# Shift operations on GpSimd instead of VectorE, two native slots in stage 0, and new engine orders, in a two-layer attention kernel

## The chip, the cores and the metric

The kernel runs on 1 core of a Trainium2 chip. The metric is the device time of one execution in microseconds (us), lower is better. Engines are named as in the profile: PE (TensorE), DVE (VectorE), ACT (ScalarE), POOL (GpSimd), SP (the queue that issues the DMAs).

## The reference

Two self-attention layers follow each other on `x` of shape 4 x 128 x 32 x 32, so 4 images of 128 channels and N = 1024 positions. Layer 1 has weights of its own and takes what layer 0 gives.

```python
q = einsum('rc,bcn->brn', Wq, xf) + bq[None, :, None]      # 16 rows
k = einsum('rc,bcn->brn', Wk, xf) + bk[None, :, None]      # 16 rows
v = einsum('oc,bcn->bon', Wv, xf) + bv[None, :, None]      # 128 rows
attn = softmax(einsum('bri,brj->bij', q, k), axis=2)       # 1024 x 1024
out = einsum('bcj,bij->bci', v, attn)
return gamma * out + x
```

## The kernel before

**Stages.** There are 8 stages: stage s is image s % 4 of layer s // 4. Stage s + 4 reads what stage s wrote to `x_all`. In a stage the 1024 x 1024 scores are made twice, in 8 tiles of 128 x 1024 each time.

**First pass (E).** `energies` (L633) makes a tile of scores with queries in the rows, `row_max` (L522) takes the negated maximum of each row on DVE, and `row_sums` (L430) takes the exponential and its row sums on ACT. `log_sums` (L436) takes the logarithm of the sums.

**The shift.** The shift of a row is its negated maximum less the logarithm of its sum. With it added to the scores, an exponential gives finished softmax weights. `cut_shift` (L527) makes it on DVE: L539 subtracts (128 x 8 elements, one column for each tile), L542 rounds the result to the short format fp32r, L544 subtracts the rounded part from the whole. The three depend on one another through semaphores. `transpose_shift` (L648) turns the two parts on PE into rows (L655), `shift_to_rows` (L546) copies them from PSUM on DVE (L553), and `place_shift` (L308) writes them by two small DMAs into spare rows of the stage's query and key tensors. In stage 0 the shift is made in two halves, of four tiles each. The first half isn't placed by a DMA but added by small matmuls (L674, L676).

**Second pass (ET).** `energies_transposed` (L657) makes the scores again, transposed and with the shift included; `attention` (L442) takes their exponential into `attn` on ACT. A tile of it is called a slot.

**Products.** Slots 0 and 7 of each stage are native: `times_v` (L713) multiplies them as fp32. Stage 0 has four native slots (0, 1, 4, 7). The other slots are cut in two fp32r parts: `hi` (a rounding, L341 on POOL or L451 on ACT) and `lo` (what the rounding left, L346 on POOL or L519 on DVE). V is cut in the same way (`v_hi`: L352 or L456, `v_lo`: L358 or L515). A cut slot then takes six fp32r passes: four in `times_v_high` (PH, L707, needs `hi`) and two in `times_v` (PV, needs `lo`). `finish` (L556) adds the residual on DVE.

**Ordering.** Each engine works through a list written out by hand: `PE_ORDER` (L46), `ACT_ORDER` (L67), `DVE_ORDER` (L81), `POOL_ORDER` (L93), `SP_ORDER` (L101). An entry is operation.stage.tile; in PE's list a last number names one of three PSUM buffers (`ring`). `warm` entries are matmuls on zeros. An engine never passes an entry that waits. Semaphores count completions, and the counts are derived from the lists. `parts.s.h` in DVE's list is a call of `cut_shift`. Stage 6 and 7 (`WHOLE`) use all 128 rows of PE in a product; the others run two products of 64 rows side by side.

The stage number stands in each entry: `ET.3.*` are the slots of stage 3 and `shift.3.1` is the transposition that they depend on. Each list interleaves two to three stages.

Of the kernel before, what the change touches and what calls it, by code (L numbers as in the profile page):

```python
# [69 lines left out]
sum.2.5 attn.0.6 v_hi.1.0 attn.0.5 sum.2.2 attn.0.7 sum.2.4 attn.1.1 attn.1.2 attn.1.3 sum.2.6 hi.1.3 sum.2.3  # L70
sum.2.1 attn.1.4 log.2.1 attn.1.0 attn.1.5 sum.3.3 attn.1.6 sum.3.7 sum.3.1 attn.2.3 sum.3.5 attn.2.1 attn.1.7
v_hi.2.0 attn.2.5 sum.3.6 sum.3.2 sum.3.0 sum.3.4 log.3.1 attn.2.2 hi.2.5 attn.2.0 sum.4.7 attn.2.4 sum.4.5 attn.2.7
attn.3.2 sum.4.2 sum.4.1 attn.3.5 attn.2.6 attn.3.7 attn.3.3 sum.4.0 sum.4.6 sum.4.3 sum.4.4 sum.5.2 log.4.1
attn.3.4 hi.3.5 attn.3.1 attn.3.0 hi.3.1 sum.5.4 sum.5.7 attn.3.6 sum.5.5 attn.4.0 attn.4.1 attn.4.2 hi.4.1 attn.4.3
sum.5.1 sum.5.6 sum.5.0 sum.5.3 hi.4.3 log.5.1 attn.4.5 attn.4.4 sum.6.6 attn.4.6 sum.6.4 attn.4.7 attn.5.0 attn.5.2
sum.6.1 attn.5.3 attn.5.1 attn.5.5 sum.6.2 sum.6.3 sum.6.7 sum.6.0 attn.5.4 sum.6.5 sum.7.5 log.6.1 sum.7.0 attn.5.6
sum.7.1 attn.5.7 sum.7.6 sum.7.4 attn.6.1 attn.6.3 attn.6.2 attn.6.4 sum.7.7 sum.7.3 attn.6.7 hi.6.1 sum.7.2 log.7.1
attn.6.0 attn.6.5 attn.6.6 hi.6.5 hi.6.6 attn.7.2 attn.7.5 hi.7.2 attn.7.6 attn.7.4 attn.7.7 hi.7.5 attn.7.3
attn.7.1 attn.7.0
# [2 lines left out]
max.0.7 max.0.3 v32.0.0 max.0.5 max.0.4 max.0.0 max.0.2 max.0.1 max.1.6 parts.0.0 max.0.6 rows.0.0 mask.2.0
stack.2.0 parts.0.1 max.1.2 rows.0.1 max.1.1 max.1.3 max.1.5 max.1.0 max.1.4 max.1.7 max.2.7 max.2.0 max.2.5
parts.1.1 v32.1.0 rows.1.1 max.2.2 finish.0.0 max.2.4 mask.3.0 stack.3.0 max.2.6 max.2.3 max.2.1 finish.0.1 v32.2.0
parts.2.1 max.3.3 rows.2.1 max.3.7 max.3.1 max.3.5 finish.1.0 mask.4.0 stack.4.0 max.3.6 max.3.2 max.3.0 max.3.4
# [715 lines left out]
```

## Time and profile before

| | us |
|---|---|
| median of 3 runs | 213.25 |
| lowest and highest | 212.74, 218.13 |
| profiled execution | 212.72 |
| span of its trace | 210.9 |
| what lies around the span | 1.8 |
| mean granted clock of PE (1 is full) | 0.984 |

The span is 1.8 us shorter than the timed execution. Times in rows are us from the start of the span. A group of instructions has its busy time, the mean of one in ns, and the idle time of the engine just before them with what ended it. A row of windows has the length of the window, then PE, PEld (PE's weight loads), DVE, ACT and POOL busy with their number of instructions, PE's granted clock as a share of full speed, DMA share and GB/s.

### The profile page before, as it was taken

How to read it: one execution, taken by the hardware profiler on the slowest of the kernel's cores; microseconds unless marked ns; L12 is line 12 of the kernel's file. 1: busy time of each engine (PE TensorE's matmuls, PEld its weight loads, DVE VectorE, ACT ScalarE, POOL GpSimd, SP SyncE). 2: the span in 40 equal slices, each digit the busy share in tenths (PEclk: the TensorE clock that was granted, in tenths of full speed). 3: DMA queues.
4: the chain of work that ended last, by engine and by line, in shares of the span. 5: the costliest groups of instructions: out<-in, count | busy, mean ns of one | idle time of the engine just before them, and what ended most of it. 6: DMA issues, size and time to landing. Idle time of an engine off the chain costs nothing.

```text
span 210.9 us, 3123 instructions
## 1 busy us (share of the span) xinstructions
PE 187.4 (89%) x1107; PEld 121.6 (58%) x1109; DVE 168.8 (80%) x162; ACT 153.3 (73%) x219; POOL 149.1 (71%) x95
## 2 busy tenths in 40 slices
...
GB/s 166 364 17 177 22 103 2 0 3 3 51 50 2 6 0 99 3 3 0 101 3 3 0 78 26 0 3 53 99 50 0 33 23 50 3 5 14 86 49 51
DMA packets 3871, 9.49 MB, mean 45 GB/s; under 512 B 545, under 2 KB 913, under 8 KB 3857
## 3 DMA queue, kind: packets, MB, share of 16 engines
...
q8 instruction: 9, 0.15, 0.3%
...
HBM read 2.89 MB, written 2.10 MB: 24 GB/s over the span
## 4 chain that ended last, share of the span: by engine, by line
PE 61%; DVE 21%; ACT 7%; issue 4%; POOL 3%; DMA 2%; SPq 0%; DVEq 0%; POOLq 0%
PE out_psum L692 25%; PE out_psum L690 5%; PE ring L667 5%; PE ring L619 5%; PE ring L643 5%; ACT ring L433 5%; DVE shift_parts L542 5%; PE ring L629 5%; DVE attn_lo L519 5%; DVE shift L539 4%; PE out_psum L693 3%; PE out_psum L726 3%; DVE shift_parts L544 3%; DVE x_all L567 2%; DVE neg_max L524 2%
## 5 line engine op out<-in xcount | busy, mean ns | idle before, releaser
L524 DVE TENSOR_REDUCE neg_max<-ring 128x1 f32<-128x1024 f32 x64 | 76.1, 1220 | 17.5 <-PE ring L645 17.1
L433 ACT ACTIVATE ring<-ring,neg_max 128x1024 f32<-128x1024 f32 x64 | 69.6, 1087 | 19.6 <-DVE neg_max L524 19.5
L346 POOL TENSOR_TENSOR attn_lo<-attn,attn_hi 128x1024 fp32r<-128x1024 f32 x34 | 81.9, 2418 | 2.6 <-ACT attn_hi L451 1.8
L445 ACT ACTIVATE attn<-ring 128x1024 f32<-128x1024 f32 x64 | 63.7, 1025 | 15.5 <-PE ring L669 13.1
L341 POOL TENSOR_SCALAR attn_hi<-attn 128x1024 fp32r<-128x1024 f32 x35 | 39.1, 1124 | 39.8 <-ACT attn L445 36.0
L643 PE MATMUL ring<-qk_swapped,qk 64*128 64x512 f32 x56 | 26.6, 481 | 3.0 <-ACT ring L433 2.4
L669 PE MATMUL ring<-qk_swapped,qk 64*128 64x512 f32 x64 | 28.0, 467 | 0.0
L667 PE MATMUL ring<-qk,qk_swapped 64*128 64x512 f32 x64 | 27.6, 461 | 0.3 <-DVE shift_rows L553 0.2
L645 PE MATMUL ring<-qk,qk_swapped 64*128 64x512 f32 x56 | 27.0, 488 | 0.0
L693 PE MATMUL out_psum<-attn,v 64*128 64x512 f32 x56 | 26.4, 591 | 0.0
L692 PE MATMUL out_psum<-attn,v 64*128 64x512 f32 x56 | 26.4, 591 | 0.0
L519 DVE TENSOR_TENSOR attn_lo<-attn,attn_hi 128x1024 fp32r<-128x1024 f32 x12 | 22.0, 1855 | 0.4 <-ACT attn_hi L451 0.4
L693 PE MATMUL out_psum<-attn_hi,v_hi 64*128 64x512 f32 x68 | 22.1, 405 | 0.0
L692 PE MATMUL out_psum<-attn_hi,v_hi 64*128 64x512 f32 x68 | 22.1, 404 | 0.0
L692 PE MATMUL out_psum<-attn_lo,v_hi 64*128 64x512 f32 x68 | 21.5, 416 | 0.0
L693 PE MATMUL out_psum<-attn_lo,v_hi 64*128 64x512 f32 x68 | 21.5, 415 | 0.0
L692 PE MATMUL out_psum<-attn_hi,v_lo 64*128 64x512 f32 x68 | 21.5, 396 | 0.0
L693 PE MATMUL out_psum<-attn_hi,v_lo 64*128 64x512 f32 x68 | 21.4, 395 | 0.0
L667 PEld LDWEIGHTS ring<-qk,qk_swapped 64*128 64x128 f32 x64 | 11.4, 188 | 11.4 <-issue 9.7
L643 PEld LDWEIGHTS ring<-qk_swapped,qk 64*128 64x128 f32 x56 | 10.8, 192 | 12.4 <-issue 10.1
L358 POOL TENSOR_TENSOR v_lo<-v,v_hi 128x768 fp32r<-128x768 f32 x8 | 16.6, 2081 | 0.7 <-ACT v_hi L456 0.6
L629 PEld LDWEIGHTS ring<-late,x_all 128*128 128x128 f32 x128 | 14.9, 191 | 3.7 <-issue 3.7
...
## 6 DMA issues: line engine op xcount, KB each, us to landing
...
qk<-shift_rows SPq DMA_DIRECT2D x7, 8.0 KB
```

The lines of the kernel that those rows point to most:

```text
L341: nc.gpsimd.tensor_scalar(attn_hi[:, k - 1], attn[:, k], 1.0, 0.0, ALU.mult, ALU.add).then_inc(cut_made["hi", "gpsimd"], 1)
L346: nc.gpsimd.tensor_tensor(attn_lo[:, k - 1], attn[:, k], attn_hi[:, k - 1].bitcast(fp32), ALU.subtract).then_inc(cut_made["lo", "gpsimd"], 1)
L433: nc.scalar.activation(e[:], e[:], ACT.Exp, bias=neg_max[s][:, i:i + 1], accum_out=row_sum[s][:, i:i + 1]).then_inc(sum_made, 1)
L445: nc.scalar.activation(attn[:, k], ring_tile("ET", s, k)[:].rearrange("p (a n) -> p a n", a=2), ACT.Exp).then_inc(attn_made, 1)
L519: nc.vector.tensor_tensor(attn_lo[:, k - 1], attn[:, k], attn_hi[:, k - 1].bitcast(fp32), ALU.subtract).then_inc(cut_made["lo", "vector"], 1)
L524: nc.vector.tensor_reduce(neg_max[s][:, i:i + 1], ring_tile("E", s, i)[:], axis=AX.X, op=ALU.max, negate=True).then_inc(max_made, 1)
L643: nc.tensor.matmul(to[:, 0:HALF], q_over_k[0:deep, rows], k_over_q[0:deep, 0:HALF], start=True, stop=True)
L645: nc.tensor.matmul(to[:, HALF:N], k_over_q[64:64 + deep, rows], q_over_k[64:64 + deep, HALF:N], start=True, stop=True).then_inc(e_mm, 1)
L667: nc.tensor.matmul(to[:, 0:HALF], k_over_q[0:64, first], q_over_k[0:64, part], start=True, stop=not added(s, h))
L669: last = nc.tensor.matmul(to[:, HALF:N], q_over_k[64:128, second], k_over_q[64:128, part], start=True, stop=not added(s, h))
L692: nc.tensor.matmul(out_psum[:, 0:HALF], v[0:64], a[0:64], start=start, stop=stop)
L693: last = nc.tensor.matmul(out_psum[:, HALF:N], v[64:128], a[64:128], start=start, stop=stop)
```

## The change

- The three shift operations are issued by GpSimd (`split_shift`) and no more by VectorE (`cut_shift`). The rounding is written as a multiplication by 1.0 with 0.0 added, as other roundings of GpSimd are. `parts` entries move from VectorE's list to GpSimd's.
- Stage 0 has two native slots (0 and 7), so its slots 1 and 4 are cut.
- The second half of stage 0's shift has a place of its own in `shift_parts` (`parts_of`).
- All five lists are written anew. In numbers of entries, before and after:

| | before | after |
|---|---|---|
| `hi` on ACT, on POOL | 11, 35 | 18, 30 |
| `lo` on DVE, on POOL | 12, 34 | 10, 38 |
| `v_hi` on ACT, on POOL | 3, 5 | 1, 7 |
| `v_lo` on DVE, on POOL | 0, 8 | 1, 7 |
| `parts` on DVE, on POOL | 9, 0 | 0, 9 |
| `PH` | 46 | 48 |
| warm-up matmuls in PE's list | 14 | 16 |

```diff
-NATIVES = [(0, 1, 4, 7), (0, 7), (0, 7), (0, 7), (0, 7), (0, 7), (0, 7), (0, 7)]
+NATIVES = [(0, 7), (0, 7), (0, 7), (0, 7), (0, 7), (0, 7), (0, 7), (0, 7)]
...
-raw.0.0.0 raw.0.1.1 QK.1.0.2 E.0.7.0 E.0.3.1 V.0.0.2 E.0.5.0 E.0.4.1 E.0.0.2 warm.0.4 E.0.2.0 E.0.1.1 E.1.6.2
-warm.0.4 E.0.6.0 warm.0.1 QK.2.0.1 shift.0.0.2 warm.0.3 ET.0.2.2 ET.0.1.0 warm.0.2 E.1.2.2 ET.0.0.1 shift.0.1.0
-PH.0.2 E.1.1.0 ET.0.3.1 E.1.3.2 PV.0.1 E.1.5.1 ET.0.4.0 E.1.0.2 PH.0.3 E.1.4.0 E.1.7.1 E.2.7.2 PV.0.3 E.2.0.0 PV.0.0
+raw.0.0.0 raw.0.1.1 E.0.7.2 E.0.0.0 QK.1.0.1 E.0.3.2 E.0.2.0 V.0.0.1 E.0.1.2 E.0.4.0 E.0.6.1 warm.0.4 E.0.5.2
+warm.0.4 shift.0.0.0 E.1.6.1 E.1.7.0 warm.0.2 QK.2.0.2 ET.0.3.1 ET.0.2.0 warm.0.1 ET.0.1.1 shift.0.1.2 E.1.2.0
+E.1.0.2 V.1.0.1 warm.0.1 ET.0.0.0 E.1.3.2 ET.0.4.1 warm.0.2 E.1.4.0 warm.0.2 E.1.5.1 PH.0.3 E.1.1.2 PH.0.2 E.2.4.0
...
-ET.7.1.1 ET.7.3.2 PH.7.6 PH.7.5 PH.7.4 PH.7.2 PV.7.7 PV.7.6 PV.7.5 PV.7.4 PH.7.1 PH.7.3 PV.7.2 PV.7.1 PV.7.3 PV.7.0
+ET.7.5.0 ET.7.4.2 ET.7.7.1 PH.7.3 PH.7.6 PH.7.1 PV.7.0 PH.7.4 PH.7.5 PV.7.1 PV.7.4 PH.7.2 PV.7.6 PV.7.2 PV.7.3
+PV.7.5 PV.7.7
...
 DVE_ORDER = """
...
-rows.7.1 lo.6.1 lo.6.6 lo.6.3 finish.6.1 finish.6.0 lo.7.2 lo.7.6 lo.7.4 lo.7.1 finish.7.1 lo.7.3 finish.7.0
+max.7.4 finish.5.1 v32.7.0 rows.7.1 lo.6.3 lo.6.4 finish.6.0 finish.6.1 lo.7.1 lo.7.3 lo.7.6 lo.7.4 finish.7.0
+finish.7.1
...
 POOL_ORDER = """
-mask.1.0 stack.1.0 v_lo.0.0 hi.0.2 lo.0.2 hi.0.3 lo.0.3 hi.0.6 lo.0.6 hi.0.5 v_lo.1.0 lo.0.5 hi.1.1 lo.1.1 hi.1.2
...
-lo.6.5 v_lo.7.0 hi.7.6 hi.7.4 lo.7.5 hi.7.1 hi.7.3
+mask.1.0 stack.1.0 v_hi.0.0 parts.0.0 parts.0.1 v_lo.0.0 lo.0.2 hi.0.3 lo.0.3 hi.0.1 v_hi.1.0 hi.0.4 v_lo.1.0
+parts.1.1 lo.0.4 hi.0.5 lo.0.5 lo.0.6 hi.1.2 hi.1.3 lo.1.2 hi.1.5 hi.1.1 lo.1.1 hi.1.6 lo.1.3 parts.2.1 lo.1.6
...
+hi.5.4 hi.5.6 v_hi.6.0 lo.5.6 lo.5.4 hi.6.1 hi.6.3 lo.6.5 parts.7.1 v_hi.7.0 lo.6.1 v_lo.7.0 lo.6.2 lo.6.6 hi.7.6
+hi.7.3 hi.7.2 hi.7.5 lo.7.2 lo.7.5
 """
 SP_ORDER = """
-swap.1.0 swap.0.0 swap.2.0 place.0.1 place.1.1 swap.3.0 place.2.1 swap.4.0 place.3.1 swap.5.0 place.4.1 swap.6.0
+swap.1.0 swap.0.0 place.0.1 swap.2.0 place.1.1 swap.3.0 place.2.1 swap.4.0 place.3.1 swap.5.0 place.4.1 swap.6.0
...
+        def parts_of(s, h):
+            return shift_parts[s][:, 2 * tiles_of(s, h).start:2 * tiles_of(s, h).stop]
...
+            def split_shift(s, h):
+                tiles = tiles_of(s, h)
+                part, count = slice(tiles.start, tiles.stop), len(tiles)
...
+                pool.wait_ge(max_made, all_of(nth_max, s, tiles))
+                pool.wait_ge(log_made, nth_log[s, h])
+                nc.gpsimd.tensor_tensor(shift[s][:, part], neg_max[s][:, part], log_sum[s][:, part],
+                                        ALU.subtract).then_inc(shift_made, 1)
+                pool.wait_ge(shift_made, nth_parts[s, h])
+                nc.gpsimd.tensor_scalar(hi, whole, 1.0, 0.0, ALU.mult, ALU.add).then_inc(shift_hi_made, 1)
+                pool.wait_ge(shift_hi_made, nth_parts[s, h])
+                nc.gpsimd.tensor_tensor(lo, whole, hi.bitcast(fp32), ALU.subtract).then_inc(shift_cut, 1)
```

## Rows read from the trace of the kernel before

**Rows 1.** The page: busy time of each engine.
```profile
PE 187.4 (89%) x1107; PEld 121.6 (58%) x1109; DVE 168.8 (80%) x162; ACT 153.3 (73%) x219; POOL 149.1 (71%) x95
```
**Rows 2.** The page: the chain that ended last, shares by line.
```profile
PE out_psum L692 25%; PE out_psum L690 5%; PE ring L667 5%; PE ring L619 5%; PE ring L643 5%; ACT ring L433 5%; DVE shift_parts L542 5%; PE ring L629 5%; DVE attn_lo L519 5%; DVE shift L539 4%; PE out_psum L693 3%; PE out_psum L726 3%; DVE shift_parts L544 3%; DVE x_all L567 2%; DVE neg_max L524 2%
```
**Rows 3.** The waits, whole span: total us, times, longest.
```profile
POOL attn_hi L341 <- ACT attn L445: 36.0, 7, 9.4
ACT ring L433 <- DVE neg_max L524: 19.5, 15, 3.4
...
PE ring L655 <- DVE shift_parts L544: 13.8, 6, 3.0
```
**Rows 4.** DVE's groups by form: the three shift operations in stages 1 to 7.
```profile
L542 DVE CAST shift_parts<-shift 128x8 fp32r<-128x8 f32 x7 | 10.0, 1429 | 0.2
...
L539 DVE TENSOR_TENSOR shift<-neg_max,log_sum 128x8 f32<-128x8 f32 x7 | 6.9, 987 | 1.3 <-ACT log_sum L440 1.1
L544 DVE TENSOR_TENSOR shift_parts<-shift,shift_parts 128x8 fp32r<-128x8 f32 x7 | 3.3, 476 | 0.2
```
**Rows 5.** Timelines around three shifts: start, duration, instruction.
```profile
27.95 1.05 POOL L341 TENSOR_SCALAR attn_hi<-attn 128x1024 fp32r<-128x1024 f32 x1 [9.41 <-ACT attn L445]
28.11 0.89 DVE L539 TENSOR_TENSOR shift<-neg_max,log_sum 128x4 f32<-128x4 f32 x1
29.07 2.34 POOL L346 TENSOR_TENSOR attn_lo<-attn,attn_hi 128x1024 fp32r<-128x1024 f32 x1
29.24 2.19 DVE L544 TENSOR_TENSOR shift_parts<-shift,shift_parts 128x4 fp32r<-128x4 f32 x1
...
46.34 0.16 DVE L539 TENSOR_TENSOR shift<-neg_max,log_sum 128x8 f32<-128x8 f32 x1
46.74 0.17 DVE L544 TENSOR_TENSOR shift_parts<-shift,shift_parts 128x8 fp32r<-128x8 f32 x1
...
131.18 0.20 ACT L440 ACTIVATE log_sum<-row_sum 128x8 f32<-128x8 f32 x1
...
135.97 0.22 PE L655 MATMUL ring<-units,shift_parts 128*16 128x128 f32 x1 [2.98 <-DVE shift_parts L544]
```
**Rows 6.** Windows: three that cover POOL's work, and two at a low clock.
```profile
28.00:113.00 85.00, 74.04 (x487) 50.56 (x488) 73.70 (x76) 69.40 (x103) 62.80 (x38) 0.98 0.11 26
113.00:163.00 50.00, 44.16 (x302) 30.58 (x300) 43.78 (x42) 39.52 (x57) 48.90 (x29) 0.99 0.12 33
163.00:202.40 39.40, 37.86 (x199) 25.93 (x198) 31.52 (x25) 27.71 (x35) 26.69 (x16) 0.97 0.08 28
...
33.00:36.00 3.00, 3.00 (x20) 2.44 (x20) 1.63 (x2) 1.74 (x4) 0.00 (x0) 0.56 0.01 3
162.00:165.00 3.00, 3.00 (x17) 2.10 (x14) 1.97 (x4) 2.60 (x4) 1.55 (x1) 0.50 0.05 11
```
**Rows 7.** POOL's groups by form, from the largest operation to the smallest.
```profile
L346 POOL TENSOR_TENSOR attn_lo<-attn,attn_hi 128x1024 fp32r<-128x1024 f32 x34 | 81.9, 2418 | 2.6 <-ACT attn_hi L451 1.8
...
L358 POOL TENSOR_TENSOR v_lo<-v,v_hi 128x768 fp32r<-128x768 f32 x8 | 16.6, 2081 | 0.7 <-ACT v_hi L456 0.6
L352 POOL TENSOR_SCALAR v_hi<-v 128x768 fp32r<-128x768 f32 x5 | 4.2, 831 | 2.9 <-DVE v L509 2.9
...
L394 POOL TENSOR_SCALAR units<-units 128x640 fp32r<-128x640 f32 x1 | 0.7, 717 | 0.0
...
L794 POOL MEMSET const-float32-0.0<- 128x1 f32 x1 | 0.1, 98 | 0.2 <-issue 0.2
```
**Rows 8.** Timeline of the end, DVE and PE.
```profile
191.74 1.99 PE L690 MATMUL out_psum<-attn_lo,v_hi 128*128 128x512 f32 x8
...
194.64 8.79 DVE L519 TENSOR_TENSOR attn_lo<-attn,attn_hi 128x1024 fp32r<-128x1024 f32 x4
...
204.01 1.21 DVE L519 TENSOR_TENSOR attn_lo<-attn,attn_hi 128x1024 fp32r<-128x1024 f32 x1
...
205.84 1.88 PE L690 MATMUL out_psum<-attn,v 128*128 128x512 f32 x4
```

116 lines of the change are left out of this document (52 added, 64 removed).

## The prediction

> **What bounds the kernel now.** I read the busy times first, then the chain that ended last, the waits, and last the timeline around the places they name.
>
> PE is busy 187.4 of 210.9 us, DVE 168.8, ACT 153.3, POOL 149.1 [rows 1]. No engine is full, so what counts is what PE waits for: 23.5 us of the span it does nothing. The chain consists of PE work for the most part, but 12% of it is DVE's three shift operations: 5% L542, 4% L539, 3% L544, some 25 us [rows 2]. Those work on 8 columns. The waits say the same from PE's side: 13.8 us in six waits of the transposition L655 for L544, up to 3.0 us [rows 3]. That is by far PE's largest wait for another engine.
>
> Why do operations on 8 columns take 1429, 987 and 476 ns in the mean [rows 4]? In stage 1, with POOL idle, the first and the last take 0.16 and 0.17 us. In stage 0, L539 starts at 28.11 during a POOL rounding that ends at 29.00 and itself ends at 29.00; L544 starts at 29.24, during POOL's `lo` that ends at 29.07 + 2.34 = 31.41, and ends at 31.43 [rows 5]. So the DVE operation stands still until the running POOL operation is over. Three dependent operations can meet three POOL operations in turn. From the end of the logarithm at 131.38 to the transposition at 135.97 it takes 4.6 us in stage 5, and PE is idle for the last 3.0 of them [rows 5].
>
> POOL is the second thing to watch. From 28 to 202.4 it is busy 62.8 + 48.9 + 26.7 = 138.4 us and idle 36.0: 22.2 before 113, 1.1 in 113 to 163, 12.7 after [rows 6]. In the middle it is 98% busy. Its idle time is waiting for `attn` (36.0 in 7 waits [rows 3], the first, 9.4, before 28 [rows 5]), and `attn` comes late where PE stood at a shift.
>
> **The change part by part.** All sums are made against the profiled execution, 212.72 us = span 210.9 + 1.8 around it; it lies 0.5 below the median of 213.25, at the low end of the runs.
>
> *1. The shift leaves DVE.* Removed from DVE are 9 x 3 operations; the seven stages with 8 columns alone are 10.0 + 6.9 + 3.3 = 20.2 us [rows 4]. DVE isn't the bound, but ACT waited 19.5 us for DVE's maxima [rows 3], so a part of this helps ACT as well.
>
> *2. The shift on POOL.* No POOL operation on 8 columns is in the trace. Upper end: the smallest ones with two inputs and with one, 2081 and 717 ns, so 2 x 2.08 + 0.72 = 4.9 us for the three. Lower end: three at the 98 ns of the one-column memset, 0.3 us [rows 7]. Between them I draw lines through two sizes: with one input 717 ns at 640 columns and 831 at 768 give 0.89 ns a column and 150 ns at none. With two inputs, 2081 at 768 contains some waiting for DVE; 2418 at 1024 gives 1.3 ns a column and then 1070 ns at none. The `lo` rows that meet no DVE operation take 2.34 [rows 5], which is 2.3 ns a column if nothing stands at none. I take 250 ns, nearest to the one-input line, since nothing says that an operation on 8 columns costs half of one on 1024. So 0.25 + 0.15 + 0.25, with 0.1 in each gap: 0.85 us. Before it come the remains of a POOL operation, some 0.8 us, half of 149.1 / 95 [rows 1]. From logarithm to transposition that is 1.7 us in place of up to 4.6, so a PE wait of 13.8 / 6 = 2.3 us nearly vanishes. I keep 0.5 for each of 7 stages. On PE: -13.8 + 3.5 = -10.3.
>
> The Trainium skill (GPSIMD Engine Reference, section 4.1, Engine selection) speaks against this move: elementwise work belongs on VectorE, GpSimd being about twice as slow with two inputs. This trace agrees for an undisturbed operation (`lo` 1.21 on DVE [rows 8], 2.34 on POOL [rows 5]). By that rule the three would cost about 1.0 us as an estimate, from 0.16 doubled, instead of 0.85: 1.4 us over nine shifts. What the rule leaves out is the standing still seen above.
>
> *3. Behind the new waits.* While POOL waits for the logarithm, the `hi` and `lo` behind it in its list stand (`parts.2.1` has `lo.1.6` behind it), and PV on PE waits for those. Before, they ran on while DVE waited. This is the cost that rival A prices. On DVE `rows` still waits for the transposition, and SP's `place` behind it; `swap.2.0` now stands behind `place.0.1`, at most the time from stacking to that shift, covered by the E tiles of stage 1 which PE has first. I put nothing for it.
>
> *4. The clock.* The granted clock was 0.56 in 33 to 36 and 0.50 in 162 to 165 [rows 6], half speed, each time after PE had waited at a shift of stage 0 or 6. That cost 3 x 0.44 + 3 x 0.5 = 2.8 us. I count 1.7 as coming back, as the start still has gaps.
>
> *5. Two slots become cut.* A native slot is four passes in 1.88 us with its tail, some 1.72 without it [rows 8]. An fp32r pass takes 0.23 at its pace (8 in 1.99, of which some 0.16 is tail), so six take 1.4 [rows 8]. So -0.7 us on PE for two. Added are two `hi` (1.05) and two `lo` (2.34) [rows 5], 6.8 us on the other engines, in the stretch where POOL idles longest (22.2 us in 28 to 113). Cover gone, they would cost at most these 6.8.
>
> *6. New lists.* POOL gets 4 `lo` more, 5 `hi` fewer, 2 `v_hi` more, 1 `v_lo` fewer and 9 shifts: 4 x 2.34 - 5 x 1.05 + 2 x 0.83 - 2.08 + 9 x 0.85 = +11.3 us. ACT gets 7 `hi` more and 2 `v_hi` fewer, 7 x 1.05 - 2 x 0.83 = +5.7. DVE loses two `lo` and gains a `v_lo`. The first loads stay as they are. The `hi` of ACT is priced as that of POOL.
>
> **The sum, from two sides.** PE's side: 210.9 - 10.3 - 1.7 - 0.7 = 198.2 of span, 200.0 us, if no new wait appears. POOL's side: of the +11.3, 2.5 (a `v_hi` and two shifts) fall before 28, so it works 138.4 + 8.8 = 147.2 us from 28 on. Behind its last entry, `lo.7.5`, follow what followed the last `lo` before, which ended at 205.22: two passes, a native slot, `finish`, the store; 210.9 - 205.2 = 5.7. With its idle time of 36.0 unchanged this is 28 + 147.2 + 36.0 + 5.7 = 216.9, so 218.7 us. But the idle time is what the stalls at the shifts made. Six waits fewer, of which about four reached POOL, at 2.3 each: -9. Work for the two cut slots in the idle start: -5. Leaves 22: 202.9 of span, 204.7 us. The later side rules. Forecast **204.7 us**.
>
> **The rivals.**
>
> *A, slower: POOL's queue.* POOL idles as long as before: what it saves where `attn` now comes earlier it loses standing at `parts` for the logarithm with work queued behind. That is the sum above, 218.7 us. For it: 98% busy in 113 to 163, and 11.3 us more work. Against it: ACT gives `attn` late because of PE's stalls, which go. It decides at an idle time of 30.0 us from 28 on, where the sum is 212.7.
>
> *B, about the same: new waits.* The stalls of PE go, but half of the gain turns into waits for `hi` and `lo`, since ACT has 5.7 and POOL 11.3 us more to do. Half of what separates 204.7 from 218.7: 211.7 us. For it: the end of the kernel, where four `lo` on DVE took 8.79 us and not 4 x 1.21 because POOL was working [rows 8]; POOL has six `lo` in the last two stages, four before. Against: the middle stages have PE at full pace but for the shifts.
>
> The Trainium skill says in Perfetto Trace Analysis, Optimizing Scalar/DVE Operations, that moving work between these two engines might not help, since they share a port. By that rule B is the case to expect; rows 5 show such a sharing, and that what it costs three short operations in a chain is more than their own time, which moving them does save.
>
> *C, faster: PE's side rules.* No new wait: 200.0 us, and 210.9 - 13.8 - 2.8 - 0.7 + 1.8 = 195.4 with all of it coming back. For it: POOL's idle total is large. Against: each list has been full of dependences, and something is next.
>
> *D: the shift on POOL is as dear as the upper end.* 4.9 in place of 0.85 us, 9 times: 36 us more on POOL, over 230 us. By the two-input line, 1.07 twice, it is 1.6 us more a shift, +15 on POOL, and 212 with half of that on the path. Only the end far from the rows of small operations gives it.
>
> **How the numbers follow.** Forecast (202 to 209): 0.50. C (below 202): 0.16. B (209 to 217): 0.22. A, with D's far end: 0.12, of which 0.09 is above 217.5. The range reaches from 199 to 213.5 and leaves some 0.05 below and 0.15 above. A measurement of this kernel can tell about 2% (4.3 us) from no change: faster than 209.0 is 0.50 + 0.16 = 0.66, within 2% 0.22 + 0.03 = 0.25, slower 0.09.
>
> **What would show it.** The wait of L655 for another engine falls from 13.8 to under 5 us, on POOL now. The three operations on POOL are 0.2 to 0.3 us each with no idle stretch of PE over 1 us at a shift. DVE's busy time falls to about 143 (20.2 and stage 0's part less, two `lo` less), POOL's rises to about 160, ACT's to 159. POOL idles about 22 us from 28 to its last entry. No window at half clock after 100. I am wrong if POOL stands at `parts` for over 1 us a stage, if the three take over 1.5 us, or if PE has new waits for `hi` or `lo` of over 6 us in sum.

## The result and the profile after

| | before | after |
|---|---|---|
| median, us (4 runs each, taken together) | 215.69 | 202.44 |
| lowest and highest | 212.74, 218.13 | 201.81, 202.95 |
| profiled execution, its span | 212.72, 210.9 | 201.81, 200.0 |
| mean granted clock | 0.984 | 0.974 |

The ratio is 0.9503, 95% interval 0.9445 to 0.9562: 5% faster. It leaves out executions of the kernel before with a disturbed clock, so it is nearer to 1 than the quotient of the medians. The forecast was 204.7 us in a range of 199 to 213.5, so time and direction came as predicted. The parts of the sum did not.

The page of the kernel after, busy time and chain by engine and by line; it answers to [rows 1, 2]:

```profile
PE 187.7 (94%) x1117; PEld 123.9 (62%) x1119; DVE 144.8 (72%) x134; ACT 157.2 (79%) x224; POOL 160.5 (80%) x122
...
POOL 40%; PE 36%; DVE 10%; issue 8%; ACT 4%; POOLq 0%; ACTq 0%
POOL attn_lo L352 25%; PE ring L649 7%; PE out_psum L698 7%; POOL attn_hi L347 7%; DVE attn_lo L546 5%; PE out_psum L732 5%; POOL v_lo L364 5%; PE out_psum L696 4%; DVE neg_max L551 4%; PE ring L625 4%; PE ring L673 3%; PE ring L635 2%; ACT ring L460 2%; PE ring L613 2%; ACT attn L472 1%
```

PE is busy as long as before (187.7 against 187.4 us) in 11 us less of span. None of the three shift lines is among the fifteen that the page names any more; the chain goes through POOL's `lo` (25%) and `hi` (7%) now. Lines have moved: L539, L542, L544 are L379, L382, L384; the transposition L655 is L661.

The waits of the kernel after (total us, times, longest), against [rows 3]:

```profile
ACT ring L460 <- DVE neg_max L551: 14.4, 13, 3.5
...
POOL attn_lo L352 <- ACT attn_hi L478: 6.7, 2, 5.1
POOL shift L379 <- ACT log_sum L467: 6.5, 2, 3.6
POOL attn_hi L347 <- ACT attn L472: 5.3, 4, 1.6
...
PE out_psum L696 <- POOL attn_lo L352: 1.1, 1, 1.1
PE out_psum L696 <- DVE attn_lo L546: 1.0, 1, 1.0
PE out_psum L698 <- DVE attn_lo L546: 0.9, 1, 0.9
...
PE ring L661 <- POOL shift_parts L384: 0.3, 1, 0.3
```

PE's 13.8 us at the shift are 0.3. POOL's 36.0 for `attn` are 5.3. Its waits for the `hi` of ACT are 6.7 where they were 1.8, and 6.5 for the logarithm are new. PE's waits for `lo` are three, 3.0 us in sum, where they were 0.7.

POOL's groups by form, and a shift in the timeline of the kernel after (start, duration, instruction), against [rows 4, 5]:

```profile
L379 POOL TENSOR_TENSOR shift<-neg_max,log_sum 128x8 f32<-128x8 f32 x7 | 2.5, 352 | 0.0
L384 POOL TENSOR_TENSOR shift_parts<-shift,shift_parts 128x8 fp32r<-128x8 f32 x7 | 1.4, 206 | 0.6
L382 POOL TENSOR_SCALAR shift_parts<-shift 128x8 fp32r<-128x8 f32 x7 | 1.4, 204 | 0.6
```

```profile
145.74 1.04 POOL L347 TENSOR_SCALAR attn_hi<-attn 128x1024 fp32r<-128x1024 f32 x1
146.75 0.20 POOL L379 TENSOR_TENSOR shift<-neg_max,log_sum 128x8 f32<-128x8 f32 x1
147.04 0.20 POOL L382 TENSOR_SCALAR shift_parts<-shift 128x8 fp32r<-128x8 f32 x1
147.33 0.21 POOL L384 TENSOR_TENSOR shift_parts<-shift,shift_parts 128x8 fp32r<-128x8 f32 x1
147.49 4.76 POOL L352 TENSOR_TENSOR attn_lo<-attn,attn_hi 128x1024 fp32r<-128x1024 f32 x2
```

The three take 0.79 us from 146.75 to 147.54, with a POOL operation directly on either side. On DVE they took 2.9 us of busy time in the mean [rows 4]. The mean of 352 for L379 comes from one of 1.19 us, which met a `lo` of DVE:

```profile
45.36 2.86 DVE L546 TENSOR_TENSOR attn_lo<-attn,attn_hi 128x1024 fp32r<-128x1024 f32 x1
47.09 1.19 POOL L379 TENSOR_TENSOR shift<-neg_max,log_sum 128x8 f32<-128x8 f32 x1
```

The `lo` ends at 48.22 and the shift's subtraction at 48.28. So the standing still works in both directions; POOL's subtraction met it once in nine shifts.

Windows of the kernel after: three that cover POOL's work from 28 us on, against [rows 6], and two in the start; behind them the same two of the kernel before:

```profile
28.00:113.00 85.00, 81.64 (x543) 54.98 (x545) 70.56 (x68) 79.61 (x119) 76.05 (x57) 0.99 0.11 27
113.00:163.00 50.00, 48.87 (x364) 38.12 (x362) 42.17 (x42) 44.67 (x65) 47.84 (x33) 1.00 0.13 39
163.00:193.80 30.80, 28.66 (x133) 19.05 (x130) 18.53 (x13) 20.39 (x23) 26.25 (x16) 1.00 0.07 27
...
12.00:15.00 3.00, 3.00 (x6) 0.94 (x4) 1.57 (x2) 2.34 (x4) 0.90 (x2) 0.55 0.00 0
24.00:27.00 3.00, 3.00 (x8) 0.90 (x8) 1.05 (x2) 1.52 (x5) 0.61 (x3) 0.50 0.59 143
```

```profile
12.00:15.00 3.00, 3.00 (x24) 2.16 (x20) 2.46 (x3) 2.08 (x3) 2.92 (x3) 1.00 0.00 0
24.00:27.00 3.00, 3.00 (x23) 1.62 (x21) 2.76 (x4) 1.97 (x6) 0.00 (x0) 1.00 0.00 0
```

POOL is busy 76.05 + 47.84 + 26.25 = 150.1 us from 28 on and idle 15.7. The two rows of the start are new and bad: the granted clock was 0.55 and 0.50, where the kernel before had 1.00 in both windows. PE's 3.00 us there hold 6 and 8 instructions where they held 24 and 23.

### The profile page after: what moved, and what is told of

Read it like the earlier page. It is cut to its first block, busy times and chain, and to the rows that moved or that the text cites. A ratio compares the mean times of both kernels' runs of the same rounds, so it can differ in the third digit from the quotient of the medians.

```text
span 200.0 us, 3150 instructions
## 1 busy us (share of the span) xinstructions
PE 187.7 (94%) x1117; PEld 123.9 (62%) x1119; DVE 144.8 (72%) x134; ACT 157.2 (79%) x224; POOL 160.5 (80%) x122
## 3 DMA queue, kind: packets, MB, share of 16 engines
q1 hardware_dynamic: 3856, 9.30, 15.7%
## 4 chain that ended last, share of the span: by engine, by line
POOL 40%; PE 36%; DVE 10%; issue 8%; ACT 4%; POOLq 0%; ACTq 0%
POOL attn_lo L352 25%; PE ring L649 7%; PE out_psum L698 7%; POOL attn_hi L347 7%; DVE attn_lo L546 5%; PE out_psum L732 5%; POOL v_lo L364 5%; PE out_psum L696 4%; DVE neg_max L551 4%; PE ring L625 4%; PE ring L673 3%; PE ring L635 2%; ACT ring L460 2%; PE ring L613 2%; ACT attn L472 1%
## 5 line engine op out<-in xcount | busy, mean ns | idle before, releaser
L352 POOL TENSOR_TENSOR attn_lo<-attn,attn_hi 128x1024 fp32r<-128x1024 f32 x38 | 94.1, 2490 | 7.3 <-ACT attn_hi L478 6.7
L551 DVE TENSOR_REDUCE neg_max<-ring 128x1 f32<-128x1024 f32 x64 | 76.1, 1220 | 18.8 <-PE ring L651 18.3
L460 ACT ACTIVATE ring<-ring,neg_max 128x1024 f32<-128x1024 f32 x64 | 69.6, 1088 | 14.9 <-DVE neg_max L551 14.4
L347 POOL TENSOR_SCALAR attn_hi<-attn 128x1024 fp32r<-128x1024 f32 x30 | 32.5, 1091 | 5.9 <-ACT attn L472 5.3
L673 PE MATMUL ring<-qk,qk_swapped 64*128 64x512 f32 x64 | 26.6, 453 | 1.2 <-ACT attn L472 0.4
L649 PE MATMUL ring<-qk_swapped,qk 64*128 64x512 f32 x56 | 25.8, 465 | 1.7 <-ACT attn L472 0.7
L675 PE MATMUL ring<-qk_swapped,qk 64*128 64x512 f32 x64 | 27.0, 459 | 0.0
L651 PE MATMUL ring<-qk,qk_swapped 64*128 64x512 f32 x56 | 26.2, 471 | 0.0
L698 PE MATMUL out_psum<-attn,v 64*128 64x512 f32 x48 | 22.5, 588 | 0.0
L699 PE MATMUL out_psum<-attn,v 64*128 64x512 f32 x48 | 22.5, 588 | 0.0
L699 PE MATMUL out_psum<-attn_hi,v_lo 64*128 64x512 f32 x72 | 22.2, 388 | 0.0
L698 PE MATMUL out_psum<-attn_hi,v_lo 64*128 64x512 f32 x72 | 22.2, 387 | 0.0
L698 PE MATMUL out_psum<-attn_lo,v_hi 64*128 64x512 f32 x72 | 20.7, 391 | 0.9 <-DVE attn_lo L546 0.9
L546 DVE TENSOR_TENSOR attn_lo<-attn,attn_hi 128x1024 fp32r<-128x1024 f32 x10 | 20.0, 2023 | 2.0 <-ACT attn_hi L478 2.0
L699 PE MATMUL out_psum<-attn_lo,v_hi 64*128 64x512 f32 x72 | 20.6, 391 | 0.0
L575 DVE SCALAR_TENSOR_TENSOR x_all<-out_psum,weights,x_all 128x512 f32<-128x512 f32 x16 | 12.0, 751 | 9.4 <-PE out_psum L696 9.0
L478 ACT CAST attn_hi<-attn 128x1024 fp32r<-128x1024 f32 x18 | 18.6, 1044 | 0.1
```

The lines of the kernel that those rows point to most:

```text
L347: nc.gpsimd.tensor_scalar(attn_hi[:, k - 1], attn[:, k], 1.0, 0.0, ALU.mult, ALU.add).then_inc(cut_made["hi", "gpsimd"], 1)
L352: nc.gpsimd.tensor_tensor(attn_lo[:, k - 1], attn[:, k], attn_hi[:, k - 1].bitcast(fp32), ALU.subtract).then_inc(cut_made["lo", "gpsimd"], 1)
L460: nc.scalar.activation(e[:], e[:], ACT.Exp, bias=neg_max[s][:, i:i + 1], accum_out=row_sum[s][:, i:i + 1]).then_inc(sum_made, 1)
L546: nc.vector.tensor_tensor(attn_lo[:, k - 1], attn[:, k], attn_hi[:, k - 1].bitcast(fp32), ALU.subtract).then_inc(cut_made["lo", "vector"], 1)
L551: nc.vector.tensor_reduce(neg_max[s][:, i:i + 1], ring_tile("E", s, i)[:], axis=AX.X, op=ALU.max, negate=True).then_inc(max_made, 1)
L649: nc.tensor.matmul(to[:, 0:HALF], q_over_k[0:deep, rows], k_over_q[0:deep, 0:HALF], start=True, stop=True)
```

## The experiments

Two theories stood first. M: the move does it, since a short DVE operation stands still until the running POOL operation ends. L: the new lists do it. Letters in the expectations are these; what other runs were for is told with each. Ratios are to the kernel before, with 95% intervals. The kernel before, measured anew beside each run, had medians of 215.6 to 216.9 us, so runs are compared with one another by their times.

**The move alone** (e1_move_alone): the lists of before, `parts` out of DVE's and into POOL's list; the second half of stage 0's shift has its own place in `shift_parts`, as in the change.

```diff
 POOL_ORDER = """
-mask.1.0 stack.1.0 v_lo.0.0 hi.0.2 lo.0.2 hi.0.3 lo.0.3 hi.0.6 lo.0.6 hi.0.5 v_lo.1.0 lo.0.5 hi.1.1 lo.1.1 hi.1.2
+mask.1.0 stack.1.0 v_lo.0.0 parts.0.0 parts.0.1 hi.0.2 lo.0.2 hi.0.3 lo.0.3 parts.1.1 hi.0.6 lo.0.6 hi.0.5 v_lo.1.0
...
-lo.6.5 v_lo.7.0 hi.7.6 hi.7.4 lo.7.5 hi.7.1 hi.7.3
+hi.5.4 hi.5.6 lo.5.4 hi.6.3 v_hi.6.0 v_lo.6.0 hi.6.2 hi.6.4 lo.6.2 v_hi.7.0 parts.7.1 lo.6.4 lo.6.5 v_lo.7.0 hi.7.6
+hi.7.4 lo.7.5 hi.7.1 hi.7.3
```

> The lists of the kernel before, with nothing changed but that the nine shift entries leave VectorE's list and stand in GpSimd's, behind the operation that GpSimd was at when the logarithm was made. Theory M (the standing still of VectorE's three short operations was the cost, and moving them is what gains): PE's wait for the transposition falls from 13.8 us in sum to under 5, and the time to 203 to 207 us. Rival L (the new lists gain, by putting more PE work between the logarithm and the transposition): the time stays at 209 to 213, since the old PE list has PE stand at the transposition in any case.

Measured: 198.83 us (198.11 to 200.26), ratio 0.9261 [0.9181, 0.934]. The page and the waits of this kernel:

```profile
PE 185.6 (94%) x1107; PEld 121.4 (61%) x1109; DVE 147.6 (74%) x135; ACT 153.5 (77%) x219; POOL 155.5 (78%) x122
...
POOL 48%; PE 26%; issue 9%; DVE 7%; ACT 6%; DMA 2%; SPq 0%; POOLq 0%
```

```profile
POOL shift L378 <- ACT log_sum L466: 12.2, 3, 5.4
...
POOL attn_hi L346 <- ACT attn L471: 6.8, 4, 2.9
...
PE ring L660 <- POOL shift_parts L383: 4.0, 3, 2.2
```

M holds, and L falls: the gain is there with the lists of before. It is 4 us more than M's range of 203 to 207 had. The move alone is worth some 14 us (198.83 against the 213.25 of the prediction's table; 16.8 against the 215.62 measured beside it) and is faster than the whole change: no execution of the one overlaps with one of the other (198.11 to 200.26, 201.81 to 202.95). The rest of the change costs 202.44 - 198.83 = 3.6 us.

**The lists alone** (e2_lists_alone): the lists and slots of after, the three operations back on DVE as `cut_shift`, each `parts` entry at a place of my choice near the same point.

```diff
-max.0.7 max.0.0 max.0.3 max.0.2 v32.0.0 max.0.1 max.0.4 max.0.6 max.0.5 rows.0.0 max.1.6 max.1.7 mask.2.0 stack.2.0
+max.0.7 max.0.0 max.0.3 max.0.2 v32.0.0 max.0.1 max.0.4 max.0.6 parts.0.0 max.0.5 rows.0.0 parts.0.1 max.1.6
...
-mask.1.0 stack.1.0 v_hi.0.0 parts.0.0 parts.0.1 v_lo.0.0 lo.0.2 hi.0.3 lo.0.3 hi.0.1 v_hi.1.0 hi.0.4 v_lo.1.0
+mask.1.0 stack.1.0 v_hi.0.0 v_lo.0.0 lo.0.2 hi.0.3 lo.0.3 hi.0.1 v_hi.1.0 hi.0.4 v_lo.1.0 lo.0.4 hi.0.5 lo.0.5
```

> The kernel after with only the move undone: its lists, with the nine shift entries taken from GpSimd's list and put in VectorE's, each at the place where VectorE was when the logarithm was made. Theory M: the three operations take 2 to 3 us a stage on VectorE again (their means 500 to 1400 ns), and 5 us or more of the gain are lost, 207 us or above. Rival L: the new PE list has 2.5 to 7 us of work between logarithm and transposition, which hides the slow chain, and GpSimd is freed of 7 us: within 2 us of the kernel after, 200 to 204.5.

Measured: 226.91 us (226.65 to 232.27), ratio 1.0555 [1.0463, 1.0647]: slower than before. DVE's groups by form and PE's waits:

```profile
L548 DVE TENSOR_TENSOR shift_parts<-shift,shift_parts 128x8 fp32r<-128x8 f32 x7 | 7.4, 1060 | 0.2
...
L543 DVE TENSOR_TENSOR shift<-neg_max,log_sum 128x8 f32<-128x8 f32 x7 | 7.4, 1056 | 1.3 <-ACT log_sum L444 1.3
L546 DVE CAST shift_parts<-shift 128x8 fp32r<-128x8 f32 x7 | 5.7, 820 | 0.2
```

```profile
PE ring L659 <- DVE v L513: 5.6, 1, 5.6
...
PE ring L659 <- DVE shift_parts L548: 4.8, 2, 2.7
```

The three take 20.5 us of DVE again, as before (20.2), distributed differently. The wait of 5.6 us is in part of my making: `parts.3.1` stood ahead of `v32.3.0` (L513, 1.2 us), which the transposition needed as well. The larger part seems to be the shift itself, whose three operations took from 97.19 to 103.35 us in that stage, and for which the transposition would have waited in either order. PE's waits have low windows of the clock behind them here (0.50 at 33 to 36, 54 to 57 and 105 to 108), and the mean clock is 0.932. How much of the 24.5 us against the changed kernel the lists owe to my placing is open. That the lists bring no gain by themselves is shown only with this placing.

**The rounding in another form** (e4_round_by_reduce): the kernel before, with L542 written as a maximum over one element, but for the first half of stage 0. It tests whether every short DVE operation stands still, or certain forms.

```diff
-                nc.vector.tensor_copy(hi, whole).then_inc(shift_hi_made, 1)
...
+                    nc.vector.tensor_reduce(hi, whole[:, :, None], axis=AX.X, op=ALU.max).then_inc(shift_hi_made, 1)
```

> The kernel before, with the rounding of the shift on VectorE (its second short operation) written as a maximum over one element instead of a copy; the same values. It has one input. If any short VectorE operation on SBUF stands still while GpSimd works, its mean stays near 1400 ns and the time at 213. If only two inputs, or the form that a copy runs in, make it stand still, its mean falls to 160 to 250 ns; the third operation then meets the GpSimd operation instead, its mean rises from 476 towards 1000 ns or more, and the time falls by 1 to 4 us only, to 209 to 212.

Measured: 211.09 us (209.5 to 211.67), ratio 0.9799 [0.9699, 0.9899]. DVE's groups by form, and the shift of stage 2 in the timelines of POOL and DVE:

```profile
L547 DVE TENSOR_TENSOR shift_parts<-shift,shift_parts 128x8 fp32r<-128x8 f32 x7 | 9.5, 1355 | 0.2
...
L539 DVE TENSOR_TENSOR shift<-neg_max,log_sum 128x8 f32<-128x8 f32 x7 | 5.2, 744 | 1.3 <-ACT log_sum L440 1.1
...
L545 DVE TENSOR_REDUCE shift_parts<-shift 128x8 fp32r<-128x8 f32 x7 | 1.1, 161 | 0.2
```

```profile
63.33 4.71 POOL L346 TENSOR_TENSOR attn_lo<-attn,attn_hi 128x1024 fp32r<-128x1024 f32 x2
...
65.78 0.16 DVE L545 TENSOR_REDUCE shift_parts<-shift 128x8 fp32r<-128x8 f32 x1
65.98 2.08 DVE L547 TENSOR_TENSOR shift_parts<-shift,shift_parts 128x8 fp32r<-128x8 f32 x1
```

The reduction takes 161 ns where the copy took 1429, on the same 8 columns in the same place. But the subtraction behind it rises from 476 to 1355 ns: it meets the POOL operation that the copy used to wait out. In the timeline the reduction passes in 0.16 us while POOL's second `lo` runs, and the subtraction ends at 68.06, with that `lo` (68.04). Of three steps that could stand still one is gone; the busy time of the three falls from 20.2 to 15.8 us. That is a test of the mechanism without moving anything, and it fits that moving all three is worth more. The Trainium skill (SBUF — State Buffer, SBUF: two separate sides) tells of an exclusive lock that GpSimd shares with VectorE operations in a two-port mode or with two SBUF inputs, held for a whole instruction. The runs agree: 1355 ns with two inputs, 161 with one in the reduction's form. The copy has one input too and stood still (1429 ns); whether it ran in such a mode no run shows.

**Two shifts made earlier** (e6_parts_earlier): e1 with two `parts` one entry earlier, where PE had waited most. It asks whether a PE wait of 4.0 us is worth removing.

```diff
-v_lo.2.0 lo.2.3 parts.3.1 hi.2.2 lo.2.2 hi.2.4 lo.2.5 v_hi.3.0 lo.2.4 hi.3.2 hi.2.6 lo.2.6 hi.3.3 v_lo.3.0 lo.3.2
-parts.4.1 lo.3.3 v_hi.4.0 hi.3.4 lo.3.1 v_lo.4.0 hi.3.6 lo.3.6 hi.4.2 lo.3.4 lo.4.1 lo.4.2 parts.5.1 lo.4.3 hi.4.5
-v_hi.5.0 hi.4.4 v_lo.5.0 hi.4.6 lo.4.4 lo.4.6 hi.5.2 hi.5.3 lo.5.3 hi.5.1 lo.5.1 hi.5.5 lo.5.2 parts.6.1 lo.5.5
...
+v_lo.2.0 lo.2.3 parts.3.1 hi.2.2 lo.2.2 hi.2.4 lo.2.5 v_hi.3.0 lo.2.4 hi.3.2 hi.2.6 lo.2.6 hi.3.3 v_lo.3.0
+parts.4.1 lo.3.2 lo.3.3 v_hi.4.0 hi.3.4 lo.3.1 v_lo.4.0 hi.3.6 lo.3.6 hi.4.2 lo.3.4 lo.4.1 lo.4.2 parts.5.1 lo.4.3
+hi.4.5 v_hi.5.0 hi.4.4 v_lo.5.0 hi.4.6 lo.4.4 lo.4.6 hi.5.2 hi.5.3 lo.5.3 hi.5.1 lo.5.1 parts.6.1 hi.5.5 lo.5.2
```

> The old lists with the shift on GpSimd, as in the run of the move alone, with two of the nine entries one or two places earlier in GpSimd's list: that of stage 4 ahead of lo.3.2, that of stage 6 ahead of hi.5.5. PE waited 1.49 and 2.25 us at those two transpositions, the second followed by 3 us at about half clock. If what is left of PE's wait for the transposition costs what it lasts, the wait falls from 4.0 to under 1.5 us and the time by 1.5 to 3 us against the run of the move alone, to 195.5 to 197.5. If GpSimd, made to stand for the logarithm, gives it back, no change: 198 to 199.5.

Measured: 199.16 us (198.72 to 201.19), no different from e1. The waits:

```profile
POOL shift L378 <- ACT log_sum L466: 13.0, 4, 5.4
...
PE out_psum L697 <- POOL attn_lo L351: 1.7, 3, 0.9
...
PE ring L660 <- POOL shift_parts L383: 0.6, 2, 0.4
```

The wait at the shift went from 4.0 to 0.6 us, waits for POOL's `lo` of 1.7 came. That fits a kernel in which POOL sets the pace and PE waits for it at one place or another.

**The shift's work on POOL doubled** (e8_shift_work_doubled): e1 with three spare operations of the same kinds ahead of each shift, whose results nothing uses.

```diff
+                nc.gpsimd.tensor_tensor(spare[0][:, part], neg_max[s][:, part], log_sum[s][:, part], ALU.subtract)
+                nc.gpsimd.tensor_scalar(spare[1][:, part], log_sum[s][:, part], 1.0, 0.0, ALU.mult, ALU.add)
+                nc.gpsimd.tensor_tensor(spare[2][:, part], neg_max[s][:, part], log_sum[s][:, part], ALU.subtract)
```

> The old lists with the shift on GpSimd, with three more short operations (8 columns, results unused) ahead of each of the nine shifts: 9 x 0.6 to 0.7 us more on GpSimd, 5.4 to 6.3 in sum, and each transposition that much later. If GpSimd's queue or the shift's latency is on the path in every stage, the time rises by 4 to 6.5 us, to 203 to 205. If there is slack at most shifts (PE had no wait at five of the eight in the run of the move alone), it rises by 1 to 3 us, to 200 to 202.

Measured: 204.97 us (202.88 to 206.82). Two of the four executions, 206.23 and 206.82, had a granted clock of 0.975 and 0.967. The other two, 202.88 and 203.72 at 0.988 and 0.989, lie 4.3 us above e1's mean of 199.0, for 9 x 0.6 = 5.4 us of added POOL work. The chain:

```profile
PE 43%; POOL 33%; DVE 7%; issue 5%; ACT 5%; DMA 4%; SPq 0%; POOLq 0%
```

Most of what is added ahead of the shifts comes out at the end. By which way isn't separated: the run lengthens POOL's queue and delays each transposition as well. PE's wait there rose from 4.0 to 5.7 us, the profiled execution has a new window at a clock of 0.56 (105 to 108 us), and POOL's share of the chain is 33%, not 48.

**Cutting the two slots alone** (e7_cut_alone): e1 with slots 1 and 4 of stage 0 cut, two `hi`, two `lo` and two PH added to the old lists.

```diff
-NATIVES = [(0, 1, 4, 7), (0, 7), (0, 7), (0, 7), (0, 7), (0, 7), (0, 7), (0, 7)]
+NATIVES = [(0, 7), (0, 7), (0, 7), (0, 7), (0, 7), (0, 7), (0, 7), (0, 7)]
```

> The old lists with the shift on GpSimd, as in the run of the move alone, and slots 1 and 4 of stage 0 cut as in the change: hi.0.1 on ACT, lo.0.1 on VectorE, hi.0.4 and lo.0.4 on GpSimd, their PH entries on PE close ahead of the PV entries, and PV.0.1 some entries later. By my sum -0.7 us of PE and nothing else, since GpSimd idles there: 198 us. Rival: the cut slots put 6.8 us of work ahead of what PE waits for and cost 1 to 3 us: 200 to 202.

Measured: 201.77 us (201.54 to 202.13), ratio 0.936 [0.9294, 0.9427], 2.9 above e1. Two windows of this kernel, and the first of them in e1:

```profile
33.00:36.00 3.00, 1.46 (x8) 1.16 (x10) 2.92 (x3) 2.53 (x6) 2.61 (x2) 0.93 0.00 0
36.00:39.00 3.00, 3.00 (x17) 2.67 (x14) 1.23 (x1) 2.18 (x5) 2.71 (x3) 0.50 0.00 0
```

```profile
33.00:36.00 3.00, 2.45 (x16) 1.21 (x14) 2.22 (x3) 3.00 (x6) 2.38 (x2) 1.00 0.00 1
```

With the two slots cut PE is busy 1.46 instead of 2.45 us in 33 to 36, where its waits are for ACT (1.2 us before the `ET` tile at 35.04), and its clock is at half in the next window. The first `finish` of stage 0 starts at 50.12 us, in e1 at 47.68; the 2.4 us are still there at 102, so the loss arises in stage 0. POOL has 3.4 us more to do there (one `hi`, one `lo`); how much of the loss is its work and how much PE's wait isn't separated.

**Four native slots in the new lists** (e3_four_natives): the changed kernel with slots 1 and 4 native again, the six entries that this frees left out.

```diff
-NATIVES = [(0, 7), (0, 7), (0, 7), (0, 7), (0, 7), (0, 7), (0, 7), (0, 7)]
+NATIVES = [(0, 1, 4, 7), (0, 7), (0, 7), (0, 7), (0, 7), (0, 7), (0, 7), (0, 7)]
```

> The kernel after with four native slots in stage 0 again (entries hi, lo and PH of slots 1 and 4 of stage 0 removed from the lists, nothing else). By my sum cutting them saved PE 0.7 us, so this is 0.7 slower at most, 203 us. Rival: GpSimd is the bound from stage 1 on, and is freed here of two hi and one lo, 4.4 us; then this is 1 to 4 us faster than the kernel after, 198.5 to 201.5.

Measured: 202.73 us (199.71 to 204.0), ratio 0.9361 [0.922, 0.9502]. Against 202.44 there is no difference that this scatter shows; one execution, at a clock of 0.991, was the 199.71. One wait of the profiled execution (204.0):

```profile
POOL attn_lo L352 <- ACT attn_hi L478: 11.4, 3, 6.5
```

POOL is busy 155.2 us here, 5.3 less than in the changed kernel, and the time doesn't fall by it: POOL's waits for ACT's `hi` grow from 6.7 to 11.4, those for the logarithm from 6.5 to 8.1. So no gain from less POOL work in stage 0 can be told in the new lists; the native slots put some 0.7 us on PE by the prediction's sum. The cut is worth nothing that could be told apart in the new lists and costs 2.9 us in the old.

**The old first entries** (e5_old_start): the changed kernel with `QK.1` back near the head of PE's list, and its evacuation first on ACT. Theory H: the half clock in the new start costs the difference.

```diff
-raw.0.0.0 raw.0.1.1 E.0.7.2 E.0.0.0 QK.1.0.1 E.0.3.2 E.0.2.0 V.0.0.1 E.0.1.2 E.0.4.0 E.0.6.1 warm.0.4 E.0.5.2
+raw.0.0.0 raw.0.1.1 QK.1.0.2 E.0.7.0 E.0.0.1 E.0.3.2 E.0.2.0 V.0.0.1 E.0.1.2 E.0.4.0 E.0.6.1 warm.0.4 E.0.5.2
...
-sum.0.7 sum.0.0 evac.1.0 sum.0.3 sum.0.2 sum.0.1 sum.0.4 log.0.0 sum.0.6 sum.0.5 log.0.1 sum.1.6 sum.1.7 attn.0.3
+evac.1.0 sum.0.7 sum.0.0 sum.0.3 sum.0.2 sum.0.1 sum.0.4 log.0.0 sum.0.6 sum.0.5 log.0.1 sum.1.6 sum.1.7 attn.0.3
```

> The kernel after, with one thing of its new start undone: the query and key projection of stage 1 (QK.1) comes again ahead of the first two score tiles on PE, and its evacuation first on ACT; the three PSUM buffers are dealt out to suit. Theory H (the new lists lose in the start: PE waits 0.9 us there where QK.1 stood before, its granted clock is 0.50 to 0.88 in much of 12 to 30 us, and stage 0 ends 4.7 us later than with the old lists): the clock stays near 1 in the start, and the time falls by 2 to 4 us, to 198.5 to 200.5. Rival T (the new lists lose in the middle or at the end): within 1 us of the kernel after, 201.5 to 203.5.

Measured: 202.8 us (201.0 to 204.24), ratio 0.9335 [0.9209, 0.946]. The two executions with the clock of the changed kernel, 0.974, took 201.0 and 201.52. A miss: the low clock from 15 to 30 us remained, so the edit didn't remove what it was to remove, and says nothing on H.

**The start fed with zeros** (e9_fed_start): the changed kernel with ten more `warm` matmuls, in gaps of PE's start.

```diff
-raw.0.0.0 raw.0.1.1 E.0.7.2 E.0.0.0 QK.1.0.1 E.0.3.2 E.0.2.0 V.0.0.1 E.0.1.2 E.0.4.0 E.0.6.1 warm.0.4 E.0.5.2
+raw.0.0.0 raw.0.1.1 warm.0.4 E.0.7.2 E.0.0.0 QK.1.0.1 E.0.3.2 E.0.2.0 V.0.0.1 warm.0.2 E.0.1.2 warm.0.2 E.0.4.0
+warm.0.2 E.0.6.1 warm.0.4 E.0.5.2 warm.0.4 shift.0.0.0 E.1.6.1 E.1.7.0 warm.0.2 QK.2.0.2 ET.0.3.1 ET.0.2.0 warm.0.1
...
```

> The kernel after, with ten more matmuls on zeros in PE's list in the start: four in the idle 0.9 us behind the first projections, two each behind V.0.0, E.0.1.2 and E.0.4.0. The last run put QK.1 first and the clock still fell at 15 to 30 us, so theory H was not tried by it. If the half clock in the start (about 3.4 us from 12.3 to 15.7 and 7 us from 22.4 to 29.8 at 0.50, some 5 us of PE work lost) is what the new lists lose, and zeros keep the clock up, the clock is near 1 there and the time falls by 1.5 to 4 us, to 198.5 to 201. If the start is paced by VectorE's maxima and the evacuations anyway, the clock rises and the time stays within 1 us of 202.4.

Measured: 199.69 us (199.48 to 200.18), ratio 0.931 [0.9188, 0.9431], mean clock 0.997. The two windows of the start, and the chain:

```profile
12.00:15.00 3.00, 3.00 (x10) 1.02 (x11) 1.52 (x2) 2.58 (x5) 0.84 (x2) 1.00 0.00 0
24.00:27.00 3.00, 2.84 (x14) 1.01 (x11) 2.21 (x3) 2.18 (x3) 0.48 (x3) 1.00 0.32 75
```

```profile
PE 46%; POOL 23%; DVE 14%; ACT 7%; issue 5%; DMA 2%; SPq 0%; POOLq 0%; DVEq 0%; ACTq 0%
```

PE's added work made the kernel 2.7 us faster, with no overlap of the executions: H holds. Of the 3.6 us between the move alone and the whole change this leaves 0.9, which the scatter doesn't tell from nothing (199.48 to 200.18 here, 198.11 to 200.26 there).

**POOL relieved at the end** (e10_tail_hi_on_act): e1 with two roundings of stage 7 moved from POOL to ACT. These two stood last in POOL's list, beside the last `lo` of DVE.

```diff
-attn.6.0 attn.6.5 attn.6.6 hi.6.5 hi.6.6 attn.7.2 attn.7.5 hi.7.2 attn.7.6 attn.7.4 attn.7.7 hi.7.5 attn.7.3
-attn.7.1 attn.7.0
...
+attn.7.7 hi.7.5 attn.7.3 attn.7.1 hi.7.1 attn.7.0 hi.7.3
...
-hi.7.4 lo.7.5 hi.7.1 hi.7.3
+hi.7.4 lo.7.5
```

> The old lists with the shift on GpSimd, as in the run of the move alone, and the last two roundings of stage 7 (hi.7.1, hi.7.3) on ACT, which is idle there, not on GpSimd, where they made four lo on VectorE take about twice 1.21 us. If the end is paced by the two engines standing in each other's way, 1 to 2 us faster, 197 to 198. If PE paces it (it had 0.7 us of waits for lo there), 0 to 0.7 us faster, 198 to 199.

Measured: 197.26 us (196.73 to 199.07), ratio 0.9204 [0.9085, 0.9322], the best of all kernels here, 1.6 below e1 and 5.2 below the change. At a clock of 1.00 the two don't overlap: at most 197.6 here, at least 198.11 in e1. The end of e1's DVE and POOL, and of this kernel's DVE:

```profile
182.18 8.80 DVE L545 TENSOR_TENSOR attn_lo<-attn,attn_hi 128x1024 fp32r<-128x1024 f32 x4
...
185.90 4.00 POOL L346 TENSOR_SCALAR attn_hi<-attn 128x1024 fp32r<-128x1024 f32 x2
```

```profile
179.87 7.11 DVE L545 TENSOR_TENSOR attn_lo<-attn,attn_hi 128x1024 fp32r<-128x1024 f32 x4
```

Four `lo` on DVE take 1.7 us less when POOL has two operations less to do beside them; those two had taken 4.00 us on POOL, where one alone takes 1.05 [rows 5]. It looks like the mechanism of the shift again, on large operations [rows 8].

## Why the prediction was right in its time and wrong in its parts

**What bounded it, and part 1: right.** PE's wait at the shift was the thing to look at. DVE's busy time fell by 24.0 us to 144.8, for a forecast of 143, and ACT's wait for DVE's maxima from 19.5 to 14.4. With the lists of before it fell to 5.1 (e1), so the new ones gave back most of that.

**Part 2, the shift on POOL: right.** Priced at 0.85 us a shift, measured 0.79; 0.25 for an operation with two inputs was 0.20, and the same with one. In the kernel after, the PE wait was 0.3 where I kept 3.5 in seven stages. With the lists of before it was 4.0. Rival D is out. The Trainium skill (GPSIMD Engine Reference, 4.1) has GpSimd about twice as slow for two inputs and roughly at line rate for one, so the prediction's estimate of 1.0 us doubled the rounding too, which that row doesn't ask for, and it was set beside a price that holds 0.2 us of gaps. Without gaps 0.61 us was measured, 0.20 for each of the three, where DVE's undisturbed subtractions took 0.16 and 0.17 [rows 5]. What counted for DVE's operations on 8 columns beside a busy POOL was the standing still.

**Part 3, POOL's new waits: nearly right.** POOL stood 6.5 us for the logarithm, in two waits, both in stage 0. In the other stages `parts` stands far enough behind in POOL's list. I wrote that over 1 us a stage would make me wrong: it was 0.8 in the mean. It was a poor sign, as the faster e1 has 12.2 us in three waits, 1.5 a stage. Rival B asked for new waits that take half of the gain; PE's for `lo` are 3.0 us.

**Part 4, the clock: the step failed.** "I count 1.7 as coming back." The low windows behind shifts did go, as predicted: no window of [rows 6]'s kind after 100 us. But the new start has its own, 0.55 at 12 to 15 and 0.50 at 24 to 27, and the mean clock fell from 0.984 to 0.974. The run with the start fed puts 2.7 us on it. I had looked at the clock where it was low before and not at what the reordered start would do to PE's feed, though the new start stood in the diff.

**Part 5, the two cut slots: the step failed.** The -0.7 us on PE was counted, and "Cover gone, they would cost at most these 6.8" was the bound. The cover wasn't there in the old lists: +2.9 us, with a PE wait for ACT and a half-clock window behind it. In the new lists it is neither gain nor loss that can be told.

**Part 6 and the sum: the terms off, and the side not proved.** I let POOL's side rule. For it: 40% of the chain is POOL's, and in the lists of before an earlier shift gives nothing (e6) and added POOL work costs most of its time (e8). Against it: in the new lists 5.3 us less on POOL gave nothing to tell (e3), and with the start fed the chain has 46% for PE and 23% for POOL (e9). Which side bounds the changed kernel stays open. By terms: 28 + 147.2 + 22 + 5.7 = 202.9 was forecast; 28 + 150.1 + 15.7 + 6.2 = 200.0 is what the span has. The idle time was the mis-sized term. I gave each of four stalls 2.3 us, the mean wait of PE, 9 in sum. In e1, which has no more than the move, POOL's idle time from 28 us to its last entry (189.9) is 161.9 - 143.6 = 18.3, so removing the stalls was worth 17.7. (Of the 36.0 before, waits for `attn` were 26.6; the first of 9.4, in the 36.0 of [rows 3], lies before 28 us.) The new lists and the cut slots took 2.6 more, where 5 were forecast for the slots. That a stall of PE delays everything behind it, ACT's `attn`, the maxima and the next stage's logarithm, would explain the size; no run shows it. The work was 2.9 more than forecast because `v_lo.0.0` (1.80 us) and the second shift of stage 0, which the sum had before 28 us, ran at 29.74 and 29.02. Rival A rested on the idle time from the other end, and is out. The errors of -6.3, +2.9 and +0.5 cancel in part, and the clock's term had the wrong sign, so that the time came within 2.3 us is luck in part; 202.44 is as near to rival C's 200.0.

**What I did not forecast at all** is the split of the gain. I worked out the change as one sum, in which the lists carried POOL's extra `lo`. The kernel with the move alone has 4 `lo` fewer on POOL, POOL busy 155.5 instead of 160.5 us, and is 3.6 us faster; e9 puts 2.7 of them on the clock of the start. Rival C's 200.0 us was nearer to that kernel than to this one.

**Open.** Behind the second `finish` of stage 5 the changed kernel takes 200.0 - 164.8 = 35.2 us and the move alone 198.5 - 164.8 = 33.7; six `lo` on POOL in the last two stages, where it had four, would explain it, but no run took those back in the changed kernel. Which side bounds that kernel, and what the loss in e7 is made of, are open too. Why the lists alone are so slow is half explained, as told there.
